# First feed-forward of a two-layer transformer: a loop with meetings becomes one unrolled stream

## The reference, cut to what matters

```python
xn = _layernorm(x)
# _L0_ffn_ref(xn): the weights are signs times a mean magnitude
bw1 = mean(|w1|, axis=1) * sign(w1)                       # 1024 x 256
h = gelu(einsum('bsd,hd->bsh', xn, bw1) + b1)
bw2 = mean(|w2|, axis=1) * sign(w2)                       # 256 x 1024
out = einsum('bsh,dh->bsd', h, bw2) + b2
# _L0_attn_ref(xn): a second layer norm, then two projections to 128 each
h2 = (xn - mu) * rsqrt(var + eps) * ln_scale + ln_bias
c_q, c_kv = h2 @ w_down_q.T, h2 @ w_down_kv.T             # "latents"
```

## Time and profile before

| | us |
|---|---|
| median of 3 runs | 2234.28 (2234.1 to 2235.52) |
| the profiled execution, its own time | 2242.25 |
| its span in the trace | 2240.6 |
| `stage_f`, until the next stage's first DMA | 277.3 |
| weights in, until the first up product | 29.5 |
| 8 batches, first transposes (28.65) to last store (268.40) | 239.8, or 30.0 each |

### The profile page before, as it was taken

One profiled execution on the slowest core, in us unless ns is written; L12 is line 12 of the kernel. 1 busy time (PEld: TensorE's weight loads), 2 busy tenths in 40 slices (PEclk: granted clock), 3 DMA queues, 4 the chain that ended last, 5 costly groups with the idle time before them and its releaser, 6 DMA issues. The chain is left out here.

```text
span 2240.6 us, 35323 instructions
## 1 busy us (share of the span) xinstructions
PE 1922.1 (86%) x12804; PEld 1333.1 (59%) x12804; DVE 1301.0 (58%) x1857; ACT 895.0 (40%) x1536; POOL 1328.1 (59%) x860
## 2 busy tenths in 40 slices
PE   5777649999999999999999964888885699998798
PEld 4666524454454545454454533666764699998798
DVE  6666436666656565666656523676663466565343
ACT  4554324433434343433434212333321355554454
POOL 2333228886868687887878632544544566666533
PEclk9888869999999999999999977999997899999899
DMA  3212231323222231323232213122213433323122
GB/s 102 75 56 75 86 106 40 76 48 95 57 67 69 50 93 34 95 48 95 57 85 58 57 29 126 32 70 77 61 57 105 133 81 81 77 51 107 29 45 42
DMA packets 81606, 158.63 MB, mean 71 GB/s; under 512 B 14496, under 2 KB 63520, under 8 KB 75552
## 3 DMA queue, kind: packets, MB, share of 16 engines
q1 hardware_dynamic: 66464, 133.40, 21.2%
q0 software_dynamic: 14592, 18.40, 5.0%
q10 hardware_dynamic: 432, 5.24, 0.6%
HBM read 80.84 MB, written 44.17 MB: 56 GB/s over the span
## 5 line engine op out<-in xcount | busy, mean ns | idle before, releaser
L916 ACT ACTIVATE a_pr<-a_pT 128x1024 f32<-128x1024 f32 x256 | 262.1, 1024 | 432.4 <-PE a_pT L739 432.4
L949 POOL TENSOR_TENSOR a_total<-a_total,a_pr 128x1024 f32<-128x1024 f32 x128 | 321.0, 2507 | 149.9 <-ACT a_pr L916 149.5
L821 DVE TENSOR_REDUCE a_row_max<-a_pG 128x2 f32<-128x1024 f32 x256 | 309.2, 1220 | 148.7 <-PE a_pG L713 148.6
L1832 DVE TENSOR_TENSOR c_h_lo<-c_h,c_h_hi 128x256 fp32r<-128x256 f32 x288 | 213.0, 757 | 195.0 <-ACT c_h_hi L1811 176.9
L752 PE MATMUL a_pA<-a_pr,a_v 128*64 128x512 f32 x1024 | 277.0, 619 | 0.1
L1811 ACT ACTIVATE c_h<-c_pU,c_b_c 128x256 f32<-128x256 f32 x288 | 138.8, 482 | 235.1 <-PE c_pU L103 234.5
L949 POOL TENSOR_TENSOR a_total<-a_pr 128x1024 f32<-128x1024 f32 x64 | 151.7, 2370 | 59.7 <-ACT a_pr L916 59.5
L930 POOL TENSOR_TENSOR a_by_cos<-a_by_cos,a_swapped 128x1024 f32<-128x1024 f32 x64 | 155.1, 2424 | 46.3 <-DMA a_swapped<-a_by_sin 46.2
L815 DVE TENSOR_TENSOR a_by_sin<-a_pG,a_sin 128x1024 f32<-128x1024 f32 x64 | 78.4, 1225 | 141.9 <-PE a_pG L103 136.9
L937 POOL TENSOR_TENSOR a_qk_lo<-a_by_cos,a_qk_hi 128x1024 fp32r<-128x1024 f32 x64 | 158.9, 2483 | 2.3 <-ACT a_qk_hi L886 2.3
L1868 POOL DMA_INDIRECT out_x<-c_y,c_ids x72 | 114.7, 1593 | 41.4 <-DVE c_y L1840 22.7
(11 more groups left out here) (248 smaller groups left out, 5072.7 us busy)
## 6 DMA issues: line engine op xcount, KB each, us to landing
a_swapped<-a_by_sin SPq DMA_DIRECT2D x256, 128.0 KB, 2.3
a_inv_by_head<-mid_inverses SPq DMA_DIRECT2D x32, 512.0 KB, 6.0
c_x_t<-mid_rows SPq DMA_DIRECT2D x37, 272.0 KB, 2.8
mid_latents<-f_c_parts SPq DMA_DIRECT2D x8, 1024.0 KB, 3.9
a_latent_parts<-mid_latents SPq DMA_DIRECT2D x8, 1024.0 KB, 7.2
d_raw<-in_weights SPq DMA_DIRECT2D x3, 2048.0 KB, 8.4
c_raw<-in_weights SPq DMA_DIRECT2D x3, 2048.0 KB, 8.1
f_x_t<-in_x SPq DMA_DIRECT2D x8, 512.0 KB, 3.9
```

The lines of the kernel that those rows point to most:

```text
L821: nc.vector.reduce_max(row_max[:, u % 2, :, t], pair[:], AX.X).then_inc(read, 1)
L916: nc.scalar.activation(pr[:, n % RP, :, :], pT[:], ACT.Exp, scale=SCALE).then_inc(exp_done, 1)
L949: nc.gpsimd.tensor_tensor(total[:, u % 2, :, :], before, pr[:, n % RP, :, :], ALU.add).then_inc(summed, 1)
L1832: nc.vector.tensor_tensor(h_lo[:, m % RH, :], h[:, m % RH, :], h_hi[:, m % RH, :], ALU.subtract).then_inc(h_lo_done[m % RH], 1)
```

## The change

`stage_f` is written anew as plain Python loops that unroll to one straight stream on each engine, with no `meet`, no `lead` and no loop in hardware. Its semaphores count upward over the whole stage; the 50 of them are cleared by DVE at the start of `stage_a` (`spent`). Buffers that cross batches are doubled or more (`x_t`, `xn`, `xT_hi`, `xT_lo`, `g_hi`, `g_lo`, `c_parts`, `y` twice, `base` three times, `out` four halves); `g` shrinks to a ring of three chunks. One more bank, `pC`, holds the latents' products. The second set of `g_hi` and `g_lo` lies where the raw weights were, so batch 1's first gelu waits for `sums_done`.

- PE's order in batch b: up chunks 0, 1; down row 0 of batch b-1; up 2, 3; latents 0; down row 1; transposes of batch b+1; up 4, 5; down row 2; latents 1; up 6, 7; `spread` of b+1; down row 3. Batch 0 has no down rows, and the sums of |w2| stand behind it; the last four down rows stand at the end.
- The second layer norm is folded away: from the first norm's variance DVE works out a combined factor (`var2`, `rstd2`, rows of 4 or 8 elements), ACT takes both roots in one instruction, POOL multiplies the identity by it (`diag`, 4 x 128x128), PE spreads it over partitions (`spread`, 4 float32 matmuls of 128 columns), ACT copies that (`cols`), and DVE multiplies the latents' product by it (`scaled`). `ln_scale` is multiplied into the weights once, `ln_bias` becomes a bias `c_bias`. Gone are the second statistics, `h`, its transposes, `hT` and POOL's split of it.
- The last add (`out`) moves from DVE to POOL; the four adds of b2 become one of 128x1024. POOL works on b+1 and on the results of b-1 and b-2. Loads of w1 come in halves with a semaphore each, x of batch 1 ahead of w2. The spare copy is issued in the middle of the stage.

```diff
+        def sem(name):
+            spent.append(st.lasting(name))
+            return spent[-1]
...
+            w2s, w2abs = raw("w2s", [P, MC, D]), raw("w2abs", [P, MC, D])
+            w1r, w1s = raw("w1r", [P, MC, D]), raw("w1s", [P, KC, FF])
+        pairs = [(sb(f"g_hi{i}", [P, MC, S], F32R), sb(f"g_lo{i}", [P, MC, S], F32R)) for i in (1, 0)]
+        g_hi, g_lo = zip(*pairs[::-1])
...
+        pC = bank("pC")
...
+                    if b == 2:
+                        sp.wait_ge(latents_out[0], 16)
+                        sp.dma_start(latent(latents, B), latent(latents, 0)).then_inc(spare_done, 16)
...
+                def spread_base(b):
+                    pool.wait_ge(norm, normed(b, ROOTS))
+                    if b:
+                        pool.wait_ge(spread_done, b)
+                    else:
+                        pool.wait_ge(ident_in, 16)
+                    for t in range(NT):
+                        nc.gpsimd.tensor_scalar(diag[:, t, :], ident[:], rstd2[:, 1, t:t + 1], None,
+                                                ALU.mult).then_inc(diag_done, 1)
+                    pool.wait_ge(norm, normed(b, XN))
+                    if b >= RB:
+                        pool.wait_ge(out_done, 2 * (b - RB) + 2)
+                    nc.gpsimd.tensor_tensor(base[b % RB][:], x_t[b % 2][:], xn[b % 2][:],
+                                            ALU.add).then_inc(sum_done, 1)
+                    if not b:
+                        pool.wait_ge(b2_in, 16 * NT)
+                    pool.wait_ge(sum_done, b + 1)
+                    nc.gpsimd.tensor_tensor(base[b % RB][:], base[b % RB][:], b2_rows[:],
+                                            ALU.add).then_inc(base_done, 1)
...
+                spread_base(0)
+                for b in range(B + 2):
+                    if b >= 2:
+                        result(2 * (b - 2) + 1)
+                    if b + 1 < B:
+                        spread_base(b + 1)
+                    if 1 <= b <= B:
+                        result(2 * (b - 1))
...
+                def roots(b):
+                    act.wait_ge(norm, normed(b, VAR2))
+                    nc.scalar.activation(std2[:], var2[:], ACT.Sqrt).then_inc(root, 1)
...
+                        if k >= RG:
+                            act.wait_ge(g_lo_done, k + 1 - RG)
+                        if k == MC:
+                            act.wait_ge(sums_done, 1)
+                            act.wait_ge(w2abs_done, 1)
+                        for dst in (g[:, k % RG, :], g_hi[b % 2][:, m, :]):
+                            nc.scalar.activation(dst, pU[k % 3][:], ACT.Gelu, bias=b1_c[:, m:m + 1],
+                                                 scale=alpha1[:, m:m + 1]).then_inc(gelu_done, 1)
+                        if not b:
+                            if m == 0:
+                                signs(1)
+                            if m == 2:
+                                columns(0)
+                            if m == 4:
+                                act.wait_ge(w2s_in, 16)
+                                nc.scalar.activation(w2abs[:], w2s[:], ACT.Abs).then_inc(w2abs_done, 1)
+                            if m == 6:
+                                nc.scalar.activation(sign2[:], w2s[:], ACT.Sign).then_inc(sign2_done, 1)
+                        if b + 1 < B:
+                            if m == 0:
+                                roots(b + 1)
+                            if m == 4:
+                                x_high(b + 1)
+                            if m == 7:
+                                columns(b + 1)
+                        if m == 5:
+                            latent_high(b, 0)
+                        if m == 7:
+                            latent_high(b, 1)
...
+                def scale(b, i):
+                    dve.wait_ge(c_done, 2 * b + i + 1)
+                    dve.wait_ge(cols_done, b + 1)
+                    if b:
+                        dve.wait_ge(c_lo_done, 2 * b + i - 1)
+                    nc.vector.tensor_tensor(scaled[i][:], pC[:], cols[b % 2][:], ALU.mult).then_inc(scaled_done, 1)
...
+                for b in range(B):
+                    for m in range(MC):
+                        k = MC * b + m
+                        dve.wait_ge(gelu_done, 2 * k + 2)
+                        if k == MC:
+                            dve.wait_ge(sign1_done, 2)
+                        nc.vector.tensor_tensor(g_lo[b % 2][:, m, :], g[:, k % RG, :], g_hi[b % 2][:, m, :],
+                                                ALU.subtract).then_inc(g_lo_done, 1)
+                        if not b and m == 2:
+                            dve.wait_ge(c_bias_made, 1)
+                            nc.vector.tensor_copy(c_bias[:], pC[:, 0:2]).then_inc(c_bias_done, 1)
+                        if b >= 2 and m == 0:
+                            weigh(2 * (b - 2) + 1)
+                        if b + 1 < B and m == 1:
+                            normalise(b + 1)
+                        if m == 3:
+                            scale(b, 0)
+                        if b and m == 4:
+                            weigh(2 * (b - 1))
+                        if m == 5:
+                            if b + 1 < B:
+                                x_low(b + 1)
+                            latent_low(b, 0)
+                        if m == 6:
+                            scale(b, 1)
+                        if m == 7:
+                            latent_low(b, 1)
+                            if b + 2 < B:
+                                moments(b + 2)
+                    if not b:
+                        dve.wait_ge(sums_done, 1)
+                        for i in range(2):
+                            nc.vector.tensor_scalar(alpha2[:, i, :], pY[0][:, 0, :], 1.0 / FF, None,
+                                                    ALU.mult).then_inc(alpha2_done, 1)
+                        dve.wait_ge(alpha2_done, 2)
...
+                def spread(b):
+                    pe.wait_ge(diag_done, NT * (b + 1))
+                    pe.wait_ge(xT_lo_done, KC * b + 1)
+                    for t in range(NT):
+                        last = nc.tensor.matmul(pT[0][:, t * P:(t + 1) * P], ones[:], diag[:, t, :],
+                                                start=True, stop=True)
+                    last.then_inc(spread_done, 1)
...
+                def down(b, m):
+                    t, half = m // 2, m % 2
+                    q = 2 * b + t // 2
+                    if t == 0:
+                        pe.wait_ge(g_lo_done, MC * b + (half + 1) * MC // 2)
+                    if not t % 2 and not half and q >= 2:
+                        pe.wait_ge(y_done, q - 1)
+                    last = halves(b, t, half)
+                    if t % 2 and half:
+                        last.then_inc(down_done, 1)
...
+                    for m in range(MC):
+                        if not b and m == MC // 2:
+                            pe.wait_ge(sign1_done, 2)
+                        if not m % 2:
+                            up(b, m)
+                            up(b, m + 1)
+                        elif b:
+                            down(b - 1, m - 1)
+                            down(b - 1, m)
...
+                        if m == 2:
+                            latents_of(b, 0)
+                        if b + 1 < B and m == 3:
+                            transposes(b + 1)
+                        if m == 5:
+                            latents_of(b, 1)
+                        if b + 1 < B and m == 6:
+                            spread(b + 1)
+                    if not b:
+                        pe.wait_ge(w2abs_done, 1)
+                        for m in range(MC):
+                            last = nc.tensor.matmul(pY[0][:, 0, :], ones[:], w2abs[:, m, :],
+                                                    start=(m == 0), stop=(m == MC - 1))
+                        last.then_inc(sums_done, 1)
+                        pe.wait_ge(sign2_done, 1)
+                        pe.wait_ge(alpha2_done, 2)
+                for m in range(MC):
+                    down(B - 1, m)
...
+                    for s in spent:
+                        dve.sem_clear(s)
```

More of the change, by code:

```diff
@@ L184, in stage_f @@
-        hT = sb("hT", [P, KC, S])
-        hT_hi = sb("hT_hi", [P, KC, S], F32R)
-        hT_lo = sb("hT_lo", [P, KC, S], F32R)
-        c_parts = sb("c_parts", [P, 4, S], F32R)
-        pX = [bank(f"pX{c}") for c in range(KC)]
+        inv_var = sb("inv_var", [P, NT])
+        share = sb("share", [P, NT])
+        var2 = sb("var2", [P, 2, NT])
+        std2 = sb("std2", [P, 2, NT])
+        rstd2 = sb("rstd2", [P, 2, NT])
+        shift = sb("shift", [P, NT])
+        xT_hi = [sb(f"xT_hi{i}", [P, KC, S], F32R) for i in range(2)]
@@ new lines, in stage_f, with raw @@
+        xT_lo = [sb(f"xT_lo{i}", [P, KC, S], F32R) for i in range(2)]
+        RG = 3
+        g = sb("g", [P, RG, S])
+        diag = sb("diag", [P, NT, P])
```

(32 more changed lines are left out.)

452 lines of the change are left out of this document (225 added, 227 removed).

## The result

| | before | after |
|---|---|---|
| median, us | 2234.19 (4 runs, 2233.41 to 2235.52) | 2160.22 (4 runs, 2154.38 to 2162.35) |
| profiled execution, us | 2242.25 | 2154.38 |
| next stage's first DMA, us | 277.31 | 202.19 |

The ratio is 0.9664 (95% interval 0.9645 to 0.9684), 74.0 us less. `stage_f` alone ends 75.1 sooner. The two profiled executions lie 87.9 apart; the other 12.8 are in stages that did not change and are not seen in the medians.

A forecast was written before the change was run, and what follows sets the result against it. It took the order of the work and its waits, no full engine, as the bound. Start 14.4, batch 0 30.6, six batches of 20.7 and the end gave 77.5 us less, minus 2 for the clock: 2159, range 2145 to 2180.

The forecast's parts named there:

- Start: Ahead of batch 0: first up product at 14.4 us, not 29.5; 1 us sooner possible without the second normalisation.
- Batch 0: First batch, holding ACT's whole preparation: 25.2 us plus 4.2 of DVE work, 30.6, so batch 1 begins at 45.0.
- 3.6 of waiting for chunk 4: ACT's wait in batch 0 for chunk 4, behind batch 1's normalisation and the first latents: 3.6 us.
- The batches: Batches 1 to 6: 20.7 us each, set by a chain of waits through DVE and POOL; 19.9 without exclusion.
- My layout: One batch laid out by its waits from PE's first up matmul, DVE's `g_lo` waiting behind POOL's adds: 20.7 us.
- PE's own work: Matmuls, transposes and `spread` of one batch summed on PE: 19.4 us, against 30.0 before.
- The end: Batch 7 at 17.5 us, then last down rows 7.4, `y` 0.85, POOL's last add 1.3; next stage's DMA at 199.8.
- Case 1: The kernel as laid out: batches of 20 to 21.5 us, time 2152 to 2168; chance 0.47.
- Case 2: PE is the bound, POOL's adds falling where DVE waits anyway: batch 19.4 to 19.9 us, 2153 or 2147; chance 0.25.
- Case 3: Every POOL add excludes DVE: batch 22.2 to 23.6 us, time 2169 to 2179; chance 0.22.
- Case 4: A never-idle PE is granted its lower clock: 38.8 us a batch, time 2299, slower than before; chance 0.03.
- Case 5: An overlooked wait on a crossing buffer takes most of the gain, stage ending near 270; chance 0.03.

The follow-up runs named there:

- e4: Changed kernel, DVE's batch 0: `c_bias` copied behind `g_lo` 0, not 2, `alpha2` made ahead of batch 2's statistics; median 2152.88 us, ratio to before 0.9636.
- e2: Changed kernel without POOL's add of b2 (128x1024) per batch, a 128x2 fill in its place; 2156.62 us, period 20.22.
- e3: Changed kernel with 4 instead of 12 matmuls for each batch's latents; 2156.02 us, period 20.49.
- e8: Changed kernel with `spread` of the next batch behind down row 3 instead of ahead of it; 2160.29 us, period 21.07.
- e14: Changed kernel with `spread` behind down row 3 and the statistics ahead of the last low part of the latents; 2164.61 us, period 20.37.
- e12: Changed kernel with DVE normalising the next x behind `g_lo` 0 instead of `g_lo` 1; 2155.84 us, periods 19.95 to 20.11.
- e7: Changed kernel in which POOL makes the add x + xn twice per batch; 2174.95 us, periods 21.5 to 23.7.
- e1: Kernel before, with `stage_f`'s hardware loop written out on every engine, meetings kept; 2230.59 us, stage end 272.68.
- e10: Changed kernel with b2's rows allocated later and a pad, so the sign matrices lie at their earlier addresses; 2159.32 us, stage end 202.79.
- e5: Changed kernel with PE doing four up chunks, then two down rows, instead of two and one; 2174.51 us, stage end 219.67.
- e9: Changed kernel with `spread` behind down row 3 and only 4 of 12 latents matmuls; 2162.58 us, steady period 20.17.

## Why the prediction was right, and where it was not

The median, 2160.22, lies 1.2 from the forecast of 2159. Its terms lie further off and cancel, so that it came this near is luck.

- **Start.** 14.4 forecast, 13.03 measured: 1.4 less, the 1 us that I had left aside for the normalisation no longer in the way.
- **Batch 0.** 30.6 forecast (its terms make 30.5), 35.05 measured, 4.5 more. The tail was right (4.2 forecast, PE stood 4.22). Two terms failed. The first chunk was to be ready after 1.1; its first gelu began after 3.4 (16.44), since PE's first matmuls came every 0.43 in place of 0.23 (the granted clock reads 1.00 from 13 to 17, so it doesn't tell why), and ACT then loaded a table (15.15, 1.28) that the sum doesn't have. The other is "3.6 of waiting for chunk 4": ACT waited 5.96. I had ACT's own work as the limit and overlooked that PE itself waits, 3.86, for `c_bias`, queued on DVE behind `g_lo` 2, and then works at a granted clock of 0.50 (26.4 to 30): the transposes at 29.13 took 1.91, not 1.09. e4 moved `c_bias` and `alpha2`, and batch 0 came to 28.9.
- **The batches.** 20.7 forecast, 20.50 measured; the six of them, from 48.08 to 171.78, 123.7 against 124.2. The number held and the step behind it did not. "`g_lo` 3 13.0, and POOL begins the add of b2": in the trace x + xn begins when `g_lo` 3 is done, since `diag`, which no row before showed, takes 0.82 and not 0.35. My layout also let `xT_lo` hang on DVE's queue alone; it hangs on PE's up 4, two gelus, `xT_hi` and gelu 5. e2 prices POOL's add at 0.28 a batch where I had 0.8 for all exclusion together; e3, e8, e14 and e12 show the chain that took its place.
- **PE's own work.** 19.4 forecast, about 19.7 by e12 (the last three periods 19.96, less the 0.26 of waiting): 64 matmuls of the down product at 0.119, not 0.11, are 0.6 more, and 44 of 512 columns at 0.232, not 0.24, 0.35 less.
- **The end.** From batch 7's first up product (171.78) to the end of POOL's last add 27.8 against 27.05; from there to the next stage 2.65 against 3.6.
- **Sum.** Stage end 202.19 against 199.8: 2.4 more, for which I had given back 2.0 for the clock, 75.5 forecast and 75.1 measured.
- **The rivals.** Case 1 by its number (20 to 21.5), by its mechanism only in part. Its range of time doesn't come out of its batches: 20 to 21.5 over seven batches is 2154 to 2165, not 2152 to 2168. Case 2, PE as the bound at 19.4 to 19.9, was 0.6 away, and e12, at 20.0, comes close to it. Case 3 isn't the kernel, but e7 shows how near it is: 2.4 more of POOL cost 1.7 a batch. Case 4: the clock is 1.00 from 52 to 172, with PE busy for 117.9 of the 120. Case 5: the stage ends at 202, not near 270.
- **Hidden as forecast.** The 50 clears: DVE's first work in the next stage stands at 214.54, released by ACT, 12.35 behind the stage's first DMA, as before (12.7).

That POOL and DVE exclude each other holds by the runs, with the numbers of e12. It is what the Trainium skill states (SBUF — State Buffer, Who interferes with whom), and the traces agree; the rule gives the length of a wait, not whether it lies on a chain, and there my layout was wrong.

Not settled: why the down product's matmuls follow each other by 0.119. The kernel before has two paces, 0.113 in rows 0 and 1 and 0.118 in rows 2 and 3, behind the transposes, and 0.113 in all four of its last batch, which has none; e1 has the same two. So the difference is 0.2 us a batch, and straight code isn't it (e1), nor are the addresses of the signs (e10). Nor is it the other compute engines: from 195.8 to 197.4 of the profile after all of them stand still, and the pace is 0.118. DMAs are busy for 0.48 of that window and aren't excluded.

Not tested: what the meetings, PE's order and the folded second norm are worth each. e1 prices the loop alone, and e5 one coarser order.

## What to carry to other kernels

When several chains of waits close within 4% of each other (here 20.5, 20.16 and PE's 19.7), a test that takes work off one engine shows nothing, and one that lengthens one thing shows too much: e2 gave 0.28 for an add of 2.7 taken away, e7 gave 1.7 for one of 2.4 put in. Follow one period from an instruction to its next instance, note the slack at each place where two chains meet, and move the producer of the tightest wait ahead of what is queued before it without need. An order that is free in the steady state should be looked at again in the first round, where engines still have their preparations: there e4 gained 6.6 us.

## What the runs showed of the hardware

- A body in a hardware loop cost 4.6 us over 7 turns against the same body written out (e1), 0.66 a turn, by one trace of each.
- An instruction of 128x4 on DVE with two SBUF inputs takes 0.16, and took 2.31 once, begun at 15.55 behind POOL's add of 128x1024 (15.49 to 17.84). So the length of POOL's instruction sets the wait, and not what DVE has to move, and the smallest lose most by ratio. In e12 one of 128x4 took 1.25 for 0.16 (at 93.98, behind POOL's add of 128x512, 93.91 to 95.20). By tile, after (duration min/median/max in ns):

```profile
L461 DVE TENSOR_TENSOR f_share<-f_mean_var,f_inv_var x8: 161/162/2314, 7.0 to 154.4; 128x4 f32<-128x4 f32 x8
```

- POOL's product of 128x128 with one factor per partition took 0.60 to 1.19, mean 0.82, where an eighth of an add of 128x1024 is 0.30.
- Gaps of PE of 1.98 (e5) and 2.08 (e7) were followed by a granted clock of 0.84 and 0.72 over 4 us. In e9 PE stood 2.13 to 2.18 at the same place in five batches: behind two of these gaps the transposes took 1.93 (76.38, granted clock 0.57 from 76 to 80) and 1.97 (158.66, 0.60 from 158.6 to 162.6), and behind the other three 1.09 (98.14, granted clock 1.00 from 98 to 102). The length of the gap alone doesn't tell.
